# A four-layer graph network: eight narrow one-hots by one operation in the count build, and the layers in pair-wide form

## What is computed

```python
x = _layernorm(x + _L0_gnn_ref(...))  # mish of sender + edge features, summed by target; MLP 128-512-128
x = _layernorm(x + _L1_gnn_ref(...))  # two rounds: relu(h @ W_self + (segment_sum(h[src], dst) / deg) @ W_neigh + b), then h / |h|
x = _layernorm(x + _L2_gnn_ref(...))  # (x / sqrt(deg_out))[src] summed by dst, @ W, / sqrt(deg_in), batch norm, relu, h / |h|
x = _layernorm(x + _L3_gnn_ref(...))  # attention over edges, 8 heads
```

## Time and profile before

| | us |
|---|---|
| median of 3 runs (lowest, highest) | 1959.26 (1959.13, 1960.12) |
| the profiled execution: its time, its span | 1961.89, 1960.2 |
| tables and preparation | 0 to 60 |
| count build, first to last item | 70 to 337 |
| message stage | 343 to 663 |
| MLP of layer zero | 671 to 746 |
| passes one, two, three | 748 to 883, 883 to 1018, 1018 to 1124 |
| all that follows | 1124 to 1960 |

### The profile page before, as it was taken

One profiled execution on the slowest core, in us unless ns is written; L12 is line 12 of the kernel. 1 busy time (PEld: TensorE's weight loads), 2 busy tenths in 40 slices (PEclk: granted clock), 3 DMA queues, 4 the chain that ended last, 5 costly groups with the idle time before them and its releaser, 6 DMA issues. The chain is left out here.

```text
span 1960.2 us, 34988 instructions
## 1 busy us (share of the span) xinstructions
PE 1366.1 (70%) x7852; PEld 1070.0 (55%) x7852; DVE 1266.2 (65%) x3530; ACT 958.8 (49%) x2139; POOL 1043.9 (53%) x985
## 2 busy tenths in 40 slices
PE   4577776899998698997999905256556665663671
PEld 2222222688887587887988802146555665652640
DVE  5899998588887457995553266355555555555635
ACT  0377677689885164442664313255444545441022
POOL 5777770577770013334643233577777777773221
PEclk9777779999999898997999957577887778776755
DMA  7467742455551164444454302588888898963101
GB/s 259 140 250 254 265 148 76 123 151 155 154 152 46 51 208 161 153 135 142 161 177 177 117 0 87 149 239 233 242 241 232 242 243 238 258 202 95 24 0 33
DMA packets 214324, 314.27 MB, mean 160 GB/s; under 512 B 31478, under 2 KB 159989, under 8 KB 214064
## 3 DMA queue, kind: packets, MB, share of 16 engines
q1 hardware_dynamic: 111376, 154.18, 24.7%
q0 software_dynamic: 33488, 81.02, 14.5%
q10 hardware_dynamic: 69328, 77.43, 12.6%
HBM read 223.87 MB, written 88.67 MB: 159 GB/s over the span
## 5 line engine op out<-in xcount | busy, mean ns | idle before, releaser
L443 POOL DMA_INDIRECT fr_ring<-table,src_i x392 | 385.5, 983 | 181.7 <-issue 116.6
L1756 POOL DMA_INDIRECT e_kv<-kv_table,e_idx x392 | 395.7, 1009 | 129.1 <-issue 119.2
L1770 PE MATMUL e_q<-e_qs,e_mask 128*128 128x136 f32 x784 | 169.5, 397 | 227.0 <-DVE e_wq L1871 192.3
L1770 PEld LDWEIGHTS e_q<-e_qs,e_mask 128*128 128x128 f32 x784 | 155.3, 291 | 233.7 <-issue 180.9
L730 PE MATMUL fe_ps<-fe_space 128*128 128x400 bf16 x591 | 201.0, 424 | 81.6 <-DVE fe_space L822 73.4
L1001 POOL CAST ly_af<-ly_au 128x3200 fp32r<-128x3200 uint16 x47 | 134.7, 2874 | 195.6 <-DVE ly_part L1340 88.8
L821 DVE TENSOR_SCALAR fe_space<-fe_space,fr_key 128x400 bf16<-128x400 f16 x591 | 202.6, 343 | 13.0 <-PE fe_ps L730 12.0
L730 PEld LDWEIGHTS fe_ps<-fe_space 128*128 128x128 bf16 x591 | 58.8, 99 | 223.7 <-issue 223.7
L1063 PE MATMUL ly_ps<-ly_af,ly_x_high 128*128 128x256 f32 (+1 forms) x650 | 167.3, 297 | 17.5 <-ACT ly_af L1161 8.0
L1868 DVE TENSOR_TENSOR e_prod<-e_q,e_kv 128x768 f32<-128x768 f32 x56 | 53.6, 958 | 171.6 <-DMA e_kv<-kv_table,e_idx 168.5
L1063 PE MATMUL ly_ps<-ly_af,ly_x_low 128*128 128x256 f32 (+1 forms) x650 | 163.9, 291 | 0.0
(11 more groups left out here) (382 smaller groups left out, 3137.2 us busy)
## 6 DMA issues: line engine op xcount, KB each, us to landing
ly_au<-edge_counts SPq DMA_DIRECT2D x88, 800.0 KB, 4.5
sums_att<-e_row ACTq DMA_DIRECT2D x56, 532.0 KB, 4.3
q_starts<-fr_ring SPq DMA_DIRECT2D x56, 476.0 KB
e_qs<-q_starts SPq DMA_DIRECT2D x56, 476.0 KB
fe_edge<-in_edgesT ACTq DMA_DIRECT2D x98, 256.0 KB
edge_counts<-fe_space ACTq DMA_DIRECT2D x25, 800.0 KB
e_drow<-dst_short SPq DMA_DIRECT2D x56, 224.0 KB
fr_ring<-table,src_i POOLq DMA_INDIRECT x392
```

The source lines that it names most:

```text
L443: pool.indirect_dma_start(f.ring[:, n % RB, t, 0:D], None, tab[0][:, :], bass.IndirectOffsetOnAxis(ap=src_i[:, at:at + 1].bitcast(U32), ax ...
L1756: pool.indirect_dma_start(kv[s][:, t, :], None, kv_table[:, :], bass.IndirectOffsetOnAxis(ap=idx[s][:, t:t + 1].bitcast(U32), axis=0)).the ...
L1770: last = nc.tensor.matmul(in_bank(ps_q, t, QW), mask[s][:, t, :], qs[s][:, t, :], start=True, stop=True)
```

## The change

In the count build the narrow one-hots of eight items are made by one tensor_tensor operation: `repeated`, a table of 128 x 8 numbers, is compared with the eight values `lo` of the items, so that the one-hot of item k is every eighth element, and PE loads its weights with that step. The `left` buffer becomes two sets of eight. `lo` is held in 16 bits. The wipes leave the tables part and the count build: the zeros lie in `space` and are written at the end of the count build, and SP issues one wipe after each slot it releases in the message stage. The ring has 50 slots. DVE waits also for the last store of the counts before it writes the zeros.

In the layers PSUM of the products holds a pair of tiles, so that the bias, near/total, relu, high, low and the small steps of the norms are made for a pair by one operation or one signal. `correct` stands before `product` of the group before. At the start of a pass PE sums most sources of the first group, then runs the product of the last group of the pass before, then most sources of the second group, and only then the last sources of the first. The out-degrees are summed four tiles later (LATE), the last four of them in pass two. `wide` lies in PSUM. The low pieces of pass two are taken at g + 5.

```diff
-RB = 52
+RB = 50
...
-SPACE = 5512
+SPACE = 6536
 AS = 3
 NG = -(-NT // 2)
 AF = 3
-XS = 4
+PS = 3
+LATE = 4
 HEAVY = 1 << 12
 NC = -(-E // HEAVY)
-ZQ, ZT = 10, 3
...
-                f.key, f.lo = held("key", [P, ITEMS]), held("lo", [P, ITEMS])
+                f.key, f.lo = held("key", [P, ITEMS]), held("lo", [P, IGS * IG], F16)
...
-        def wipe(sp, f, n):
-
-            zero = f.ring[:, RB - 2:RB, :, :].rearrange("p n t f -> p (n t f)")[:, 0:TB * QW]
-            sp.dma_start(q_starts[n * BW:(n + 1) * BW, :].rearrange("(p t) f -> p (t f)", p=P), zero).then_inc(wiped, 16)
-
...
-                        sp.wait_ge(zeroed, 1)
-                        for n in range(ZQ):
-                            wipe(sp, f, n)
...
+                        dve.memset(f.lo[:, ITEMS:], 0.0)
+                        after(dve.tensor_copy(f.lo[:, 0:ITEMS], ps_a[:, 0:ITEMS]), "lo_out")
...
+                def lefts(g):
+                    return space[:, g * (IG * P // 2):(g + 1) * (IG * P // 2)].bitcast(BF16).rearrange("p (e k) -> p e k", k=IG)
+
+                def left(n):
+                    return lefts(n // IG % 2)[:, :, n % IG]
...
+                repeated = space[:, after_hot + NW // 2:after_hot + NW // 2 + IG * P // 2].bitcast(F16).rearrange("p (e k) -> p e k", k=IG)
...
+                zero = space[:, SPACE - TB * QW:SPACE]
...
-                        for j in range(-(-(NB - ZQ) // ZT)):
-                            sp.wait_ge(c["taken"], 16 + 8 * j)
-                            for n in range(ZQ + j * ZT, min(ZQ + (j + 1) * ZT, NB)):
-                                wipe(sp, f, n)
+                        sp.wait_ge(ready, 4)
+
+                        def wipe(n):
+                            sp.dma_start(q_starts[n * BW:(n + 1) * BW, :].rearrange("(p t) f -> p (t f)", p=P), zero).then_inc(wiped, 16)
+
                         for n in range(RB, NF):
                             sp.wait_ge(c["item_n"], sp.value_load(f.free_at[0:1, n - RB:n - RB + 1], min_val=1, max_val=FI))
                             sp.sem_inc(released, 1)
+                            wipe(n - RB)
+                        for n in range(NF - RB, NB):
+                            wipe(n)
                         for k in range(2):
                             sp.wait_ge(stored[k], (NT + 1 - k) // 2 * 16)
+                        sp.wait_ge(wiped, NB * 16)
...
-                            if n == RB - 2:
-                                pool.wait_ge(wiped, NB * 16)
...
-                                nc.tensor.matmul(ps[:, bass.ds(at, NW)], left(n % IS), right(n % IS),
+                                nc.tensor.matmul(ps[:, bass.ds(at, NW)], left(n), right(n % IS),
...
+                        dve.tensor_copy(repeated, iota[:, :].unsqueeze(2).broadcast_to([P, P, IG]))
...
-                            dve.tensor_scalar(right(s), numbers, f.key[:, bass.ds(n, 1)], None, ALU.is_equal)
-                            dve.tensor_scalar(left(s), numbers[:, 0:P], f.lo[:, bass.ds(n, 1)], None, ALU.is_equal).then_inc(c["hot"], 1)
-
-                        for n in range(IS):
-                            hot(n, n)
-                        with dve.Fori(1, ITEMS // IS) as r:
-                            for k in range(IS):
-                                dve.wait_ge(c["item"], r * IS + (k + 1 - IS))
-                                hot(r * IS + k, k)
-                        for n in range(ITEMS // IS * IS, ITEMS):
+                            dve.tensor_scalar(right(s), numbers, f.key[:, bass.ds(n, 1)], None, ALU.is_equal).then_inc(c["hot"], 1)
+
+                        def hot_left(n, g):
+
+                            dve.tensor_tensor(lefts(g), repeated, f.lo[:, bass.ds(n, IG)].unsqueeze(1).broadcast_to([P, P, IG]), ALU.is_equal)
+
+                        for n in range(2 * IG):
                             c.free(dve, "item", n, IS)
+                            if n % IG == 0:
+                                hot_left(n, n // IG)
+                            hot(n, n % IS)
+                        with dve.Fori(1, ITEMS // (2 * IG)) as r:
+                            for k in range(2 * IG):
+                                dve.wait_ge(c["item"], r * 2 * IG + (k + 1 - IS))
+                                if k % IG == 0:
+                                    hot_left(r * 2 * IG + k, k // IG)
+                                hot(r * 2 * IG + k, k % IS)
+                        for n in range(ITEMS // (2 * IG) * 2 * IG, ITEMS):
+                            c.free(dve, "item", n, IS)
+                            if n % IG == 0:
+                                hot_left(n, n // IG % 2)
                             hot(n, n % IS)
 
                         dve.wait_ge(c["item"], ITEMS)
                         dve.wait_ge(c["taken"], 8 + BLOCKS)
                         dve.wait_ge(stored[1], NT // 2 * 16)
-                        dve.wait_ge(wiped, NB * 16)
-                        dve.memset(ring[:, RB - 2:RB, :, D:RW1], 1.0).then_inc(ready, 1)
+                        dve.wait_ge(stored[0], (NT + 1) // 2 * 16)
+                        dve.memset(zero, 0.0).then_inc(ready, 1)
...
-                bank = [st.enter_context(nc.psum_tensor(f"ly_ps{k}", [P, BANK], F32)) for k in range(7)]
+                bank = [st.enter_context(nc.psum_tensor(f"ly_ps{k}", [P, BANK], F32)) for k in range(8)]
...
+                wide = bank[7][0:NC, 0:2 * P]
...
+                def in_degrees(m):
+
+                    return LATE <= m < NT + LATE
+
                 def counts_free(eng, m):
 
                     g = group(m) - AF
                     if g >= 0:
                         c.ready(eng, "agg", g)
-                        if g < NG:
-                            c.ready(eng, "deg", tiles(g)[-1])
+                        for k in tiles(g):
+                            if in_degrees(k):
+                                c.ready(eng, "deg", k - LATE)
...
-                    return min(g + 4, NG + AF - 1) if g < NG else min(g + 6, 2 * NG + AF - 1)
+                    return min(g + 4, NG + AF - 1) if g < NG else min(g + 5, 2 * NG + AF - 1)
+
+                def early(g):
+
+                    return NT - 2 if g // NG == 1 else NT - 1 - NS
...
-                            for m in tiles(g):
-                                c.ready(pool, "high", m)
-                                if m < NT:
-                                    c.ready(pool, "h", m)
-                                    pool.tensor_tensor(h_low[:, m, :], h(m), h_high[:, m, :].bitcast(F32), ALU.subtract).then_inc(c["low"], 1)
-                                else:
-                                    j = m - NT
-                                    pool.tensor_tensor(x_low[:, j, :], xs[j % XS][:, :], x_high[:, j, :].bitcast(F32), ALU.subtract).then_inc(c["low"], 1)
+                            c.ready(pool, "high", g)
+                            if g < NG:
+                                c.ready(pool, "h", g)
+                                pool.tensor_tensor(planes(h_low, g), hs(g), planes(h_high, g).bitcast(F32), ALU.subtract).then_inc(c["low"], 1)
+                            else:
+                                scaled = xs[g % 2][:, 0:len(tiles(g)), :].rearrange("p t f -> p (t f)")
+                                pool.tensor_tensor(planes(x_low, g), scaled, planes(x_high, g).bitcast(F32), ALU.subtract).then_inc(c["low"], 1)
...
-                                elif g % NG == 0:
-                                    c.ready(pe, "low", (g // NG - 1) * NT + a)
+                                elif g % NG == 0 and a % 2 == 0:
+                                    c.ready(pe, "low", g - NG + a // 2)
...
+                            here = ps_h[g % 2]
+                            if g >= 2:
+                                c.ready(pe, "sum" if g < 2 * NG + 2 else "h2", g - 2 if g < 2 * NG + 2 else g - 2 - 2 * NG)
+                            if g < 2 * NG:
+                                row, w_neigh, w_self = weights[g // NG]
+                                for k in range(2):
+                                    nc.tensor.matmul(here[:, 0:width(g)], ones_r[0:1, :], bias[0:1, g // NG, k:k + 1, :].broadcast_to([1, len(tiles(g)), D]), start=(k == 0), stop=False)
+                                c.ready(pe, "at", g)
+                                for i in range(len(tiles(g))):
+                                    nc.tensor.matmul(here[:, i * D:(i + 1) * D], aT(g, 1)[:, i * P:(i + 1) * P], wm[:, w_self, :], start=False, stop=(i == len(tiles(g)) - 1))
+                                left_out(pe, g)
+                                for i in range(len(tiles(g))):
+                                    last = nc.tensor.matmul(here[:, (2 + i) * D:(3 + i) * D], aT(g, 0)[:, i * P:(i + 1) * P], wm[:, w_neigh, :], start=True, stop=True)
+                            else:
+                                left_out(pe, g)
+                                for i in range(len(tiles(g))):
```

(33 more changed lines are left out.)

## The result

The changed kernel takes 1936.27 us (median of 4 runs) beside 1959.69 for the kernel before: 23.4 us less, a ratio of 0.988 with a 95% interval of 0.986 to 0.991. The forecast was 1918 in a range of 1900 to 1943, so it lies in the range and on the right side, but little more than half of the forecast gain came. The two profiled executions differ by 26.2 us (spans 1960.2 and 1934.0).

| stretch | before | after | difference | forecast |
|---|---|---|---|---|
| start to first item | 70.1 | 71.3 | +1.2 | +1.7 |
| count build, first to last item | 268.9 | 257.8 | -11.1 | -13 |
| to the first message step | 4.0 | 4.2 | +0.2 | 0 |
| message stage | 315.5 | 320.9 | +5.4 | +3.5 |
| to the first aggregation (MLP) | 89.9 | 92.2 | +2.3 | 0 |

The account below looks back on a forecast made before the run. TensorE's order was taken to bound count build, message stage and pass two, a DVE and POOL loop pass one. Terms 0 + 0 - 13 + 1.7 + 2.5 + 1 - 18.8 - 1.8 - 6 - 8.2 = -42.6 gave 1918 us, range 1900 to 1943.

Parts of the forecast that it names:

- my bounds of nothing and 0.20: Count build, weight load with a step: cost between nothing and a load of 0.20 us (+56 if not hidden); taken as 0.
- the bound that left part of the slowing to the gathers: Count build, wipes moved out: -8 instead of -13 us if POOL's gathers and not wipes cost half.
- The wait for the store: Message stage start: DVE waits for the last store of the counts, first work about 349.1 instead of 346.66, +2.5 us.
- wipes +1: Message stage: 48 wipes, one per 2.65 us step, add 180 GB/s to 139; +1 us, bounds 0 and +20.
- First boundary: Between passes one and two: 37.3 us becomes 31.3, -6 (0 to -12), with about 6 waiting for the low piece.
- the one that said the stretched operation goes with `wide`: Pass one: `wide` in PSUM cuts the choice from 3.02 to about 0.4 us; TensorE then bounds at 8.67 a group, -18.8.
- My line for the full stall, +7: Pass two: +7 us instead of -1.8 if the four late out-degrees on DVE stall fully.
- Second boundary: Between passes two and three: POOL has less ahead of the low piece, 27.7 becomes about 19.5 us, -8.2 (-3 to -12).
- A: Rival, layers: they give only 15 of 34 us, as pair-wide signals release nothing until both tiles are done; 1937, chance 0.20.
- B: Rival, message stage: wipes slow TensorE's word reads and POOL's gathers, costing 10 to 20 us; 1933, chance 0.13.
- C: Rival, count build: the stepped load isn't hidden, 0.095 us longer for each of 591 items, +56; 1974, chance 0.08.
- D: Rival, better than forecast: hiccups in the 3.475 go, boundaries fill up entirely, DVE idles less; 1902, chance 0.10.

Follow-up runs that it names:

- singles: Changed kernel with the narrow one-hots made one by one for each item, without a step; ratio 0.991 to the kernel before, count build 465.0 us against 462.5.
- best1: Changed kernel with relu and roots of pass two in PSUM and no late out-degrees; ratio 0.980 to the kernel before, passes 328.2 us against 357.0.
- relu_roots_psum: Changed kernel with pass two's relu result and norm roots in PSUM, late sums kept; ratio 0.984 to the kernel before, passes 336.6 us against 357.0.

## Why the prediction was right or wrong

**The number.** 1936 lies in the range but 18 us from the forecast of 1918, and there by some luck: the rows that the change touches sum to -21.3, half of the -42.6, and -7.2 came from stages that it doesn't touch.

**Count build, right.** One operation for eight: no gain, and *singles* agrees. The load with a step is hidden, though it did get longer, 0.143 for 0.097, between my bounds of nothing and 0.20. The Trainium skill's "SBUF — State Buffer", section "Door 1: The DMA port swizzle", has each access to a new line of 16 bytes pay, and the longer load agrees. That it costs nothing here is shown by the 0.33 from load to load. Moving the wipes gave -11.1 of -13: groups took 3.53 us on average, not 3.475. In the quiet end of before POOL was busy 26.9 of 73 us, in the whole build of the changed kernel 166.9 of 258, so the bound that left part of the slowing to the gathers deserved weight.

**Message stage, mis-sized.** +5.4 for +3.5. The wait for the store was right in kind; of its +2.5 the first `least` shows +1.2, and the first eight steps together +2.5. The term "wipes +1" measured +2.9 in one execution, or +4.2 if the rest of the first eight steps is counted with it, and the cause wasn't shown.

**Pass one, right mechanism, two terms mis-sized.** The choice leaves the cast, and TensorE becomes the bound. But the period is 8.14, not 8.67. I took only the bias from the product. It takes 0.32 us for a pair, which is 0.41 saved. But the four self and four neighbour matmuls in rows take 0.55 + 0.36 = 0.91, where the two tiles had 2.01 - 0.73 = 1.28, and `correct` takes 0.34 instead of 0.43: 0.41 + 0.37 + 0.09 = 0.87 in all. That, and the order at the start of the pass, made -26.1 of -18.8.

**First boundary, right.** 31.2 us for 31.3, and the wait is for low pieces, as forecast. That it is right to 0.1 is luck: the waits are 2.60 and 5.05 us, 7.65 for about 6, and all the rest 23.5 for 25.

**Pass two, wrong.** I put the late out-degrees at +2 and the pair-wide norms at nothing, and forecast -1.8; it was +13.9 over eleven groups, although the shorter product alone is worth 11 × 0.89 = -9.8. So 23.7 us were lost. TensorE's waits make 17.6 of them, and the other 6 go with its granted clock, 0.91 here against 1.00 before. The step that failed is the one that said the stretched operation goes with `wide`, and with it the small steps of the norms for a pair at nothing. I had seen one operation wait for a cast and treated it as that operation's trait. The residual has it too, and the trace of before held that: the residual of one tile (line 1361) took 0.35 us at least and 2.54 at most there. The maximum got it by the change itself: over one element it stayed at 0.16 beside casts, over two it took up to 2.52. Not every operation that reads SBUF alone has it: beside casts the reciprocals of the norms stayed at 0.17, the statistics at 0.30 and the reductions at 3.48. In pass two before, TensorE waited for nothing; at 9.02 a group VectorE had time for its stretched residuals. After the change three things met: a period of 8.14, up to four casts in a row in pass two because POOL catches up behind the late sums (it idled 5.62 us before them, for a late sum), and the sums of 3.5 us each. Two experiments split it: without late sums -10.0, without the stretch -20.4, with both -28.8, which is nearly the sum of 30.4. My line for the full stall, +7, was half of the +13.9.

**Second boundary, wrong.** -8.2 forecast, +0.9 measured, -5.0 in *best1* and in *relu_roots_psum*, which has the late sums. So 6 of the 9 us missing failed through the same step, since the last low pieces stand behind norms that stand behind stretched residuals; the other 3 are gain that I put too high.

**The rivals.** A came closest: the layers were to give 15 of 34 and gave 17, with 1937 for 1936. But the reason that I wrote (signals for pairs release nothing until both tiles are done) isn't what held; with pairs unchanged, *best1* has no wait in pass two. B shows 4.2 us at most, not 10 to 20. C is excluded by the steps. D didn't come.

## What to carry to other kernels

Where one operation is stretched by another engine's work, moving the operand of that one operation doesn't cure the rest. List all operations of the engine that can meet a long GpSimd operation, by their minimum and maximum times, and see which will be on the path once the bound gets faster. Look again after widening one: the maximum was safe over one element and not over two. Work that is moved one stage on must be priced with the queue that it meets there: four sums of 3.5 us cost 10 us in pass two, and where they came from they cost 1.4, at the boundary. When a step removes a wait and the next bound is TensorE, count its matmuls in rows: the self and neighbour products of two tiles took 0.91 us back to back and 1.28 tile by tile.

## What the runs showed of the hardware that was not expected

A maximum over 2 elements a partition took 2.52 us and a residual of 128 elements up to 2.97 us while GpSimd cast 3200 elements in 2.86; with their tensor, or one of two, in PSUM they never exceeded 0.17 and 0.352 us. The same maximum over one element never exceeded 0.16 beside casts. The Trainium skill, "SBUF — State Buffer", says in the section "Who interferes with whom" that a VectorE instruction with two SBUF inputs contends with a GpSimd instruction that reads SBUF, and that `tensor_scalar` can contend in its faster modes, where the one that comes second blocks fully. The residual agrees with and without PSUM. The maximum and the choice are `tensor_scalar` and agree by their times; in which mode they ran no trace shows. Reductions of 3200 elements from SBUF kept to 3.46 to 3.49 us throughout.

The operation of 128 x 8 one-hots took 0.69 us with the eight values innermost and 1.23 with them outermost, on the same 1024 elements.

On chip 7 the same kernel takes 27% longer than in the comparison, and nothing of it lies in the passes: 357.0 against 356.3 us.
